# Relative attention: position scores only for keys nearer than the clip distance

## The reference

```python
MAX_REL = 68
idx = clip(r[None, :] - r[:, None], -MAX_REL, MAX_REL) + MAX_REL   # [query, key]
rk2 = rel_k[idx]                                # one 16-vector for each (query, key)
attn1 = einsum('bhqd,bhkd->bhqk', rq, rk)       # content scores, rk = x @ Wk + bk
attn2 = einsum('bhqd,qkd->bhqk', rq, rk2)       # position scores
attn = softmax((attn1 + attn2) / sqrt(128))
out = (einsum('bhqk,bhkd->bhqd', attn, rv) + einsum('bhqk,qkd->bhqd', attn, rel_v[idx])) @ Wo + bo
```

## Time and profile before

| | us |
|---|---|
| median of 3 runs | 2060.26 (2059.11 to 2060.94) |
| the profiled execution, its own time | 2057.68 |
| its span (first to last instruction) | 2055.9 |
| PE busy over the span | 1715.7 (83%) |
| DVE busy | 1438.6 (70%) |
| ACT busy | 928.4 (45%) |
| POOL busy | 828.1 (40%) |
| L1684, position scores, PE busy | 140.1 |

### The profile page before, as it was taken

One profiled execution on the slowest core, in us unless ns is written; L12 is line 12 of the kernel. 1 busy time (PEld: TensorE's weight loads), 2 busy tenths in 40 slices (PEclk: granted clock), 3 DMA queues, 4 the chain that ended last, 5 costly groups with the idle time before them and its releaser, 6 DMA issues. The chain is left out here.

```text
span 2055.9 us, 59079 instructions
## 1 busy us (share of the span) xinstructions
PE 1715.7 (83%) x21927; PEld 1411.4 (69%) x21927; DVE 1438.6 (70%) x3464; ACT 928.4 (45%) x2319; POOL 828.1 (40%) x1677
## 2 busy tenths in 40 slices
PE   4999999999888856991599999999999999857640
PEld 3888888888667746991477777777777777634420
DVE  5777777777668854665477888888888888644323
ACT  2211111121177614771366766667667666414320
POOL 2333333333014664661002443434444444447771
PEclk9999999999999967996699999999999999979875
DMA  8900000000040012222133333333333333335537
GB/s 300 133 0 0 0 0 0 0 0 0 1 174 14 30 35 59 70 72 90 32 58 63 77 73 71 70 72 73 73 75 79 74 75 72 89 114 151 154 99 253
DMA packets 312955, 147.80 MB, mean 72 GB/s; under 512 B 205142, under 2 KB 291572, under 8 KB 312308
## 3 DMA queue, kind: packets, MB, share of 16 engines
q1 hardware_dynamic: 300164, 118.58, 24.8%
q0 software_dynamic: 12544, 25.91, 3.9%
HBM read 72.23 MB, written 73.37 MB: 71 GB/s over the span
## 5 line engine op out<-in xcount | busy, mean ns | idle before, releaser
L1939 ACT ACTIVATE rel_e<-rel_s_ps,rel_neg_max 128x255 f32<-128x255 f32 x512 | 199.9, 479 | 47.8 <-DVE rel_neg_max L2192 47.1
L2192 DVE TENSOR_REDUCE rel_neg_max<-rel_s_ps 128x4 f32<-128x1020 f32 x128 | 156.2, 1221 | 91.7 <-PE rel_s_ps L1684 88.9
L524 PE MATMUL tok_main_ps<-tok_w_h,tok_feat_h 128*128 128x512 f32 x512 | 204.6, 400 | 0.9 <-DVE tok_feat_low L99 0.9
L524 PE MATMUL tok_main_ps<-tok_w_h,tok_feat_l 128*128 128x512 f32 x512 | 200.1, 391 | 0.0
L524 PE MATMUL tok_main_ps<-tok_w_l,tok_feat_h 128*128 128x512 f32 x512 | 199.8, 390 | 0.0
L84 POOL TENSOR_TENSOR tok_q_pre<-tok_v_q,tok_v 128x128 f32 (+1 forms) x32 | 38.8, 1214 | 306.0 <-DVE tok_q L273 291.7
L1705 PEld LDWEIGHTS rel_t_ps<-all_k_ident,rel_e 128*128 128x128 f32 x1024 | 110.5, 142 | 70.0 <-issue 64.7
L1668 PE MATMUL rel_s_ps<-rel_k_h,rel_q_head_h 128*128 128x256 f32 x512 | 156.7, 306 | 0.0
L1705 PE MATMUL rel_t_ps<-all_k_ident,rel_e 128*128 128x128 f32 x1024 | 139.7, 280 | 16.5 <-issue 11.7
L1668 PE MATMUL rel_s_ps<-rel_k_l,rel_q_head_h 128*128 128x256 f32 x512 | 146.2, 285 | 0.0
L1668 PE MATMUL rel_s_ps<-rel_k_h,rel_q_head_l 128*128 128x256 f32 x512 | 146.1, 285 | 0.0
(11 more groups left out here) (374 smaller groups left out, 4633.9 us busy)
## 6 DMA issues: line engine op xcount, KB each, us to landing
rel_q_rep<-q_rows SPq DMA_DIRECT2D x256, 64.0 KB
o_rows<-rel_rv SPq DMA_DIRECT2D x256, 64.0 KB
x_slots<-early_zeros SPq DMA_DIRECT2D x16, 520.0 KB, 6.5
exp_x<-x_slots SPq DMA_DIRECT2D x32, 260.0 KB
y_rows<-early_zeros SPq DMA_DIRECT2D x16, 512.0 KB, 6.5
final_y<-y_rows SPq DMA_DIRECT2D x16, 512.0 KB, 10.3
exp_x<-x_slots SPq DMA_DIRECT2D x72, 65.0 KB, 1.9
rows_y<-y_rows SPq DMA_DIRECT2D x8, 512.0 KB, 6.9
```

Source lines behind the costliest of these rows:

```text
L524: nc.tensor.matmul(main_ps[s][:, cols], feat[fk][:, s, j, :], w_p[wk][:, j, cols], start=(j == 0 and (fk, wk) == (0, 0)), stop=False)
L1939: last = nc.scalar.activation(e[u % 2][:, n, 0:L], s_ps[u % 2][:, n, 0:L], ACT.Exp, bias=neg_max[u % 2][:, n:n + 1])
L2192: nc.vector.tensor_reduce(neg_max[u % 2][:], s_ps[u % 2][:, :, 0:L], AX.X, ALU.max, negate=True)\
```

## The change

The position table has its first row subtracted from it (`ktab` minus `first_key`). So its entries are zero for every key that lies 68 or more places behind the query, and what was subtracted is added to the keys: `bk_near` is the bias of the keys plus the first row. A position score is then made only for the columns `lo:hi` of a block, where the keys are nearer than the clip distance. Behind the query nothing is needed past the clip. Ahead of it, all queries of unit 0 share the last row from key 131 on, and all of unit 1 from key 195 on (`KR`). There the key array of that unit holds the key with the last row (`bk_far`) instead of the first. So there are three key arrays: for unit 0, for unit 1, and a plain one for units 2 and 3. Each key tile grows from 256 to 3 x 256 columns, and it is filled by five instructions instead of one, on ACT and again on DVE: 3 x 131, 2 x 64, 61, 64 and 2 x 61 columns.

```diff
+KR = [GQ * u + GQ + MAX_REL - 1 for u in range(2)]
...
-        k_p = [[m.sb(f"k{r}_{k}", [P, T], FP32R) for k in "hl"] for r in range(2)]
+        k_p = [[m.sb(f"k{r}_{k}", [P, 3, T], FP32R) for k in "hl"] for r in range(2)]
+        first_key, bk_near, bk_far = (m.sb(n, [P, 1]) for n in ("first_key", "bk_near", "bk_far"))
...
+        def key_parts(near, far):
+
+            return ((slice(0, 3), slice(0, KR[0]), near), (slice(1, 3), slice(KR[0], KR[1]), near),
+                    (slice(2, 3), slice(KR[1], T), near),
+                    (slice(0, 1), slice(KR[0], KR[1]), far), (slice(0, 2), slice(KR[1], T), far))
...
-                                             k_p[r][kk][:],
+                                             k_p[r][kk][:, min(u, 2), :],
...
-                                off = KOFF - BQ * (UB * u + n) - QUAD * c
+                                q0 = BQ * (UB * u + n)
+                                lo, hi = max(0, q0 - MAX_REL + 1), KR[u] if u < 2 else L
+                                off = KOFF - q0 - QUAD * c
                                 last = nc.tensor.matmul(
-                                    s_ps[u % 2][32 * c:32 * c + 32, n, 0:L],
+                                    s_ps[u % 2][32 * c:32 * c + 32, n, lo:hi],
                                     q_pos[r][64 * f:64 * f + 64, 8 * u + 4 * k + c].rearrange("p h i -> p (h i)"),
-                                    ktab[64 * f:64 * f + 64, off:off + L], start=False, stop=True,
+                                    ktab[64 * f:64 * f + 64, off + lo:off + hi], start=False, stop=True,
...
                 def head():
                     weights.wait(pe)
+                    pe.wait_ge(key_ready, 1)
...
-                    nc.scalar.activation(k_p[r][0][:], pa, ACT.Identity, bias=bk_sb[:]).then_inc(kh_ready, 1)
+                    for units, cols, bias in key_parts(bk_near, bk_far):
+                        n = [P, units.stop - units.start, cols.stop - cols.start]
+                        last = nc.scalar.activation(k_p[r][0][:, units, cols], pa[:, cols].unsqueeze(1).to_broadcast(n),
+                                                    ACT.Identity, bias=bias[:])
+                    last.then_inc(kh_ready, 1)
...
-                    nc.vector.scalar_tensor_tensor(k_p[r][1][:], pa, bk_sb[:], k_p[r][0][:].bitcast(FP32),
-                                                   ALU.add, ALU.subtract).then_inc(kl_ready, 1)
+                    for pair, cols, bias in key_parts(bk_near, bk_far):
+                        n = [P, pair.stop - pair.start, cols.stop - cols.start]
+                        last = nc.vector.scalar_tensor_tensor(
+                            k_p[r][1][:, pair, cols], pa[:, cols].unsqueeze(1).to_broadcast(n), bias[:],
+                            k_p[r][0][:, pair, cols].bitcast(FP32), ALU.add, ALU.subtract)
+                    last.then_inc(kl_ready, 1)
...
+                    nc.vector.tensor_tensor(bk_near[:], bk_sb[:], ktab[:, 0:1], ALU.add)
+                    nc.vector.tensor_tensor(bk_far[:], bk_sb[:], ktab[:, KWIN - 1:KWIN], ALU.add)
+                    link(nc.vector.tensor_copy(first_key[:], ktab[:, 0:1]))
+                    nc.vector.tensor_scalar(ktab[:], ktab[:], first_key[:], None, ALU.subtract).then_inc(key_ready, 1)
```

More of the change, by code:

```diff
@@ L1507, in relative_attention @@
         p1, p3 = ([s_ps[j][:, 2 * k:2 * k + 2, :].rearrange("p n k -> p (n k)") for j in range(2)] for k in range(2))
+        key_ready = m.sem("key_ready")
         s_up, s_gate_ready, s_half_ready, s_hid_ready, s_down, s_added = (m.sem(n) for n in (
@@ L2051, in head @@
                     act.wait_ge(ready, 3)
+                    act.wait_ge(key_ready, 1)
                     act.wait_ge(zeroed, 4)
```

## The result

The changed kernel takes 2078.59 us (median of 4 runs, 2073.52 to 2081.5), the kernel before 2060.28 beside it (4 runs, 2059.11 to 2060.94): ratio 1.0083, interval 1.0063 to 1.0103. It is slower, by 18.3 us where 13.7 was forecast (2074.0, range 2057 to 2092). The profiled execution of after has 2078.14 us, 20.5 more than that of before.

The account below looks back on a forecast made before the run. ACT, DVE and PE were each taken to bound parts of a batch. +0.33 us a batch (+10), start +5.5, end -1.5 made +14: 2057.68 to 2071.7, plus 2.6 for the median, 2074 us; range 2057 to 2092.

Parts of the forecast that it names:

- PE 94% busy and yet not the bound: Relative attention, 1010 to 1740 us: PE busy 94%, but its remaining pauses, where ACT and DVE finish, decide.
- D: Batch part from the end of unit 3's position scores to L1705 (now L1716): 5.66 us, bound by ACT.
- Two of four savings count: Position scores: only unit 3's 0.45 and unit 1's 0.22 us pay; DVE hides unit 2's, ACT unit 0's.
- ACT's addition: Five key instructions instead of one on ACT: 1.36 us against 0.38, so +1.0 us a batch.
- R3: Rival: dearer broadcast, ACT +1.9 us or DVE over 2.4; +1.2 a batch, about 2104 us; chance 0.12.
- R2: Rival: small ACT instructions are cheap, +0.5 us; -0.17 a batch, about 2058 us; chance 0.15.
- DVE's addition: Five key remainders on DVE instead of one: 1.70 us, +1.26, hidden inside ACT's delay within a batch.
- Where PE stands: PE pauses about 1.0 us before the queries' projection, for DVE, and 0.8 to 1.0 before L1716 of unit 3.
- B: Batch part from L1749 (now L1760) to the router's matmul L1778: 6.01 us, bound by DVE, no saving.
- Start of the stage: Unhidden key work in batches 0 and 1, 4.5 us, plus preparing the table on DVE, 1.0: +5.5 us.
- The loop: +0.33 us a batch over 30 batches, +10, less 1.5 for the last two batches, which make no keys.
- R4: Rival: closely spaced PE pauses lower the granted clock for some batches; about 2110 us; chance 0.03.

Follow-up runs that it names:

- the last pair: Low side alone narrowed with the router's row moved, against the kernel before: 2038.23 us; the same with the table's two-tensor subtraction behind the first x: 2032.65 us.

## Why the prediction was right

- **PE 94% busy and yet not the bound.** Right. The decisive reading was that D lasts until ACT frees the tile, which the trace calls only "issue". The run with the narrow matmuls alone kept D, and the one with the key arrays alone lengthened it by 1.04.
- **Two of four savings count.** Right: -0.50 and -0.27 for -0.45 and -0.22. The slope of 0.84 ns a column and pass carried well: unit 3 went from 1.09 to 0.62 (-0.47 for -0.45), unit 1 to 0.84 (-0.25 for -0.22).
- **ACT's addition.** Right in mechanism and size: five instructions in 1.37 us for 1.36 worked out, by the pace of the neighbour with the same operands. The slope of 0.86 ns a column that it used is in no pair of its rows (from 0.38 for 256 columns to 0.59 for 512 it is 0.82, and from L1955's 0.36 it is 0.90), but either would have given 1.33 to 1.39. The 3D broadcast out of PSUM cost nothing that can be seen beside this sum. So R3 (+1.9) and R2 (+0.5) are out: +0.99 came.
- **DVE's addition.** The five take 1.50 us from the first start to the last end (1230.35 to 1231.85), where the prediction had 1.75: +1.0 over the 0.48 of before, for +1.26. It was mis-sized by some 0.25, without effect inside the loop.
- **Where PE stands.** Wrong. The prediction had PE stall 1.0 before the queries' projection, for DVE. It stands 0.61 before L1760, one step earlier, for ACT's L1977, which the five instructions push back as well; I had followed ACT's chain only to its last link and not asked who waits for the ones between. Beside it the wait for DVE is hidden. Once ACT's share was gone, it came out at 0.70 where predicted. The total of D did not depend on it. The wait before the router's matmul is 0.62 to 0.73 where 0.9 to 1.2 was expected: B kept its 6.01, and PE spends the rest of its slack earlier, 0.50 before the turn of unit 2. The same oversight about ACT's chain hid a gain: the router's two instructions stand ahead of L1961 too, and moving them took 0.46 from D.
- **Start of the stage.** +6.2 for +5.5. The keys cost 4.1 for 4.5. The table cost 2.1 for 1.0: the step that failed is the price of its subtraction. 0.87 of it is what the two-tensor form costs too (11.64 - 10.77), the other 1.26 the wait beside GpSimd's memset. The 0.87 is itself a difference: on DVE the small operations and the two-tensor subtraction take 1.17 us more ahead of L2397, the old L2388 (1003.75 to 1004.98, where the kernel before has 975.44 to 975.50), and 0.30 comes back, because x is then normalized behind the last big memset and takes 0.60 instead of 0.90.
- **The rest of the 4.6 us between forecast and result.** The loop gave 9.3 for 8.5 (10 - 1.5): the steady 0.31 over the batches, about 2.4 us more in two irregular ones (25.67 at 1371.98, 25.44 at 1422.27, described below), less the end. Without those two the loop would have given 6.9, so part of the closeness of 9.3 to 8.5 is luck. 4.5 of the profiled difference lay ahead of the stage and belongs to that execution; how much of the median's 18.3 is such spread, these runs can't tell.
- **The clock** did not move: 0.99 at 89% busy (R4).

## What to carry to other kernels

When a group of matmuls gets shorter, find for each of its places the engine that ends that part; only the places where PE itself ends it pay, and an engine with room in the average can have none there. A step that one engine does once and another waits for is dear to multiply: look for the form in which all users share it (here one side of the clip goes into a bias for all units, and keeps 0.55 of the 0.74 us a batch that the narrow matmuls alone bring, at no price in the loop). Follow the whole chain of the engine that you load, and ask of every link who waits for it: that shows both where the new wait sits and what can be moved out of its way.

## What the runs showed of the hardware that I had not expected

**A DVE operation that waits for GpSimd's memset.** TENSOR_SCALAR over 512 fp32 columns took 1.97 us beside memsets, against 0.69 for TENSOR_TENSOR at the same place. It ended at 976.58, 0.28 after the end of the memset that was running when it began (976.30), and the next memset, which had started at 976.24, took 2.08 instead of 1.80. So each held the other up. From these rows I estimate that the operation itself needs about 0.3, the time from the memset's end to its own. The Trainium skill (SBUF — State Buffer, Who interferes with whom) says that DVE and GpSimd share one pair of ports under an exclusive lock, that tensor_scalar can enter a mode that takes this pair, and that a DVE operation with two inputs in SBUF contends with a GpSimd instruction that reads SBUF, not with one that only writes it, as a memset does; by that rule the first form waits and the second does not, and the traces agree. The normalization of x ahead of PE's first turn shows the same in the kernel before: 0.90 us at 980.48, ending 0.15 after the last big memset (981.23), where beside no memset it takes 0.60.

**Pauses of PE in and after GpSimd's indirect transfers.** Every second batch GpSimd issues eight DMA_INDIRECT in 10 us. In five traces (of the changed kernel, the moved row, the low side with the moved row, and of the last pair), every pause of PE over 0.5 us in the loop that does not repeat from batch to batch began inside such a stretch or within 4.3 us of its end, always between 1350 and 1520 us of the kernel, in a group of equal matmuls with no semaphore between them, as the one above (1.53 us, 4.1 after the stretch). The trace of the key arrays alone has one of 0.94 us that began 5.1 after its stretch. The one profiled execution of the kernel before shows none. On the chip where it takes 2214 us this is a large effect: from 1180 us on, every batch with such a stretch takes about 31.3 us and every other one 23.4, against 22.95 and 23.4 for the same loop elsewhere. There PE breaks off like this (the kernel with the subtraction behind x):

```profile
1407.32 0.65 PE L1723 MATMUL rel_t_ps<-attn_value_table,rel_eT 128*32 128x64 f32 x15
1408.59 0.32 PE L1723 MATMUL rel_t_ps<-attn_value_table,rel_eT 128*32 128x64 f32 x2 [0.62 <-issue]
1410.01 1.43 PE L1723 MATMUL rel_t_ps<-attn_value_table,rel_eT 128*32 128x64 f32 x44 [1.09 <-issue]
```

and its granted clock over 1015 to 1740 us is 0.91 instead of 1.00. What PE lacks in these pauses is not shown: the trace names no releaser. The page of the profile lists two DMA queues of the kind "instruction" (157 and 90 packets, 3.3 MB together). One packet of 16 KB starts on the first of them for every 250 to 253 instructions of PE and PEld, in the middle of the stage every 5.6 to 6.3 us. Each pause over 0.5 us inside a group of equal matmuls, in all eleven profiles of changed kernels on the faster chips, began between 0.2 us before and 1.0 us after the landing of such a packet, and that packet had started 6.0 to 11.0 us after the one before it (in the changed kernel the pause at 1381.94 beside a landing at 1382.01, and the one at 1432.24 beside 1431.89). So instructions that come late behind GpSimd's and SP's transfers would fit. This is a coincidence in time and no proof: the kernel before has intervals up to 9.2 us and no pause, and no run here changed the transfers alone.
